# Adding an attention bias with accumulating transfers from DRAM instead of GpSimd additions

## The reference

```python
qkv = in_proj_weight[None] * x[:, None, :, :, :, None] + in_proj_bias[None]
q, k, v = (qkv[:, n].reshape(16, -1, 4) for n in range(3))
q, k = softplus(q), softplus(k)
s = cumsum(k[:, :, :, None] * v[:, :, None, :], axis=1)
z = cumsum(k, axis=1)
y = einsum('nsi,nsij->nsj', q, s) / einsum('nsi,nsi->ns', q, z)[:, :, None]
y = concatenate([ones_like(y[:, :1]), y[:, :-1]], axis=1)
y = sum(hid_proj_weight[None] * y[:, None], axis=-1) + hid_proj_bias[None]
y = sum(out_proj_weight[None] * tanh(y), axis=1) + out_proj_bias[None]
```

## Time and profile before

| | |
|---|---|
| median of 3 runs | 3651.82 us (3649.66 to 3657.69) |
| the profiled execution's own time | 3653.92 us |
| its span | 3652.1 us |
| busy in the span | PE 2039.0 us, DVE 1541.7, ACT 852.6, POOL 1682.0 |
| of POOL: the gathers of the second layer | 1089.1 us |
| of POOL: bias additions (line 956), 16 for each of the three parts | 72.7, 72.6 and 72.5 us |
| first and last projection of a value in the last stage | start at 2523.8 and 3524.9 us |
| granted clock of TensorE, mean | 0.758 of full speed |

### The profile page before, as it was taken

How to read it: one execution, slowest core, us unless ns; L and a number is a source line. 1 busy time by engine, 2 the same in 40 slices (tenths; PEclk the granted TensorE clock), 3 DMA queues, 4 the chain that set the end, 5 groups by cost and what they waited for, 6 DMA issues and landing times. The chain is left out here.

```text
span 3652.1 us, 36691 instructions
## 1 busy us (share of the span) xinstructions
PE 2039.0 (56%) x14480; PEld 1282.6 (35%) x14480; DVE 1541.7 (42%) x1349; ACT 852.6 (23%) x1117; POOL 1682.0 (46%) x1342
## 2 busy tenths in 40 slices
PE   3666323444544444444534444561788888888887
PEld 2544212222232222232322223351454544544545
DVE  3222420221122202220222112374788888878885
ACT  3111301021111112021111111252333233233241
POOL 0000075555655565555655575233454554554542
PEclk9877656666766666666766676786899899999899
DMA  7999442333323232323323232203111311212212
GB/s 322 431 432 431 155 114 83 89 89 89 92 84 91 85 96 85 92 84 91 91 83 92 84 97 84 100 17 105 55 61 55 103 60 66 95 57 67 96 52 78
DMA packets 169913, 423.39 MB, mean 116 GB/s; under 512 B 92648, under 2 KB 111232, under 8 KB 152704
## 3 DMA queue, kind: packets, MB, share of 16 engines
q1 hardware_dynamic: 114560, 271.53, 20.2%
q0 software_dynamic: 55296, 151.07, 13.8%
HBM read 396.91 MB, written 25.58 MB: 116 GB/s over the span
## 5 line engine op out<-in xcount | busy, mean ns | idle before, releaser
L436 POOL DMA_INDIRECT gath<-table,idx x1152 | 1089.1, 945 | 798.9 <-PE p_col L594 348.6
L594 PE MATMUL p_col<-ident,gath 128*128 128x128 f32 x2304 | 398.9, 338 | 667.2 <-issue 440.0
L594 PEld LDWEIGHTS p_col<-ident,gath 128*128 128x128 f32 x2304 | 342.8, 177 | 736.6 <-issue 632.4
L537 DVE TENSOR_TENSOR xt<-xt,p_y 128x512 f32 (+1 forms) x16 | 11.0, 688 | 1380.8 <-remote 1363.0
L483 ACT ACTIVATE cols<-p_col 128x384 f32<-128x384 f32 x384 | 186.0, 491 | 1162.1 <-remote 557.6
L582 PE MATMUL p_y<-cols,wreg 128*64 128x512 f32 x576 | 306.4, 692 | 141.2 <-issue 86.0
L535 DVE TENSOR_TENSOR gath<-gath,p_stat 128x2304 f32<-128x2304 f32 x128 | 317.5, 2549 | 64.4 <-DMA gath<-table,idx 62.6
L1192 PE MATMUL p_state<-xt,tri 128*128 128x512 f32 x512 | 257.4, 650 | 64.5 <-DVE prod L1080 64.5
L960 POOL TENSOR_TENSOR query<-query,expo 128x2048 f32<-128x2048 f32 x16 | 102.1, 6379 | 334.7 <-DVE query L1058 334.7
L1080 DVE TENSOR_TENSOR prod<-p_state,query 128x2048 f32<-128x2048 f32 x80 | 183.1, 2289 | 127.5 <-PE p_state L1197 127.5
L1228 PE MATMUL p_sum<-ident,prod 128*128 128x128 f32 x1024 | 171.0, 337 | 107.2 <-DVE prod L1102 107.2
(11 more groups left out here) (221 smaller groups left out, 2772.6 us busy)
## 6 DMA issues: line engine op xcount, KB each, us to landing
ring<-in_w SPq DMA_DIRECT2D x64, 2304.0 KB, 18.8
hidw<-in_hidw SPq DMA_DIRECT2D x64, 1024.0 KB, 4.8
gath<-table,idx POOLq DMA_INDIRECT x1152
table<-pix SPq DMA_DIRECT2D x256, 64.0 KB, 1.8
xt<-in_x SPq DMA_DIRECT2D x1, 4096.0 KB, 12.7
ring<-in_x SPq DMA_DIRECT2D x1, 4096.0 KB, 12.9
resid<-xt SPq DMA_DIRECT2D x32, 128.0 KB, 2.4
xlate<-resid SPq DMA_DIRECT2D x16, 256.0 KB, 2.9
```

Of the source, the lines that this page charges most:

```text
L436: nc.gpsimd.indirect_dma_start(out=gath[:, t % SLOTS, k].rearrange("p n c -> p (n c)"), out_offset=None, in_=entries[u], in_offset=bass.In ...
L594: last = nc.tensor.matmul(p_col[g][:, k], corners, ident[:], start=(r == 0), stop=(r == 1), is_transpose=True)
```

## The change

The bias is no longer kept in SBUF. `add_bias` becomes a transfer issued by POOL which reads the bias from DRAM and adds it to the tile where it lies. Each part gets a counter of its own that rises by 16 per transfer, and a counter `bias_begun` is raised by POOL ahead of each transfer.

```diff
-EARLY = {"inw": [P, 3 * ATT, HALF], "inb": [P, 3 * ATT, HALF]}
+EARLY = {"inw": [P, 3 * ATT, HALF]}
...
             def add_bias(part, n, scaled, b, done):
                 pool.wait_ge(scaled, b + 1)
-                tt(part[:], part[:], inb[:, n * A:(n + 1) * A], ALU.add).then_inc(done, 1)
+                pool.sem_inc(bias_begun, 1)
+                pool.dma_start(part[:], d["inb"][:, n * A:(n + 1) * A], accum_op=ALU.add).then_inc(done, 16)
...
                 add_bias(value, 2, v_scaled, b, v_ready)
-                add_bias(key, 1, k_scaled, b, biased)
-                add_bias(query[u], 0, q_scaled, b, biased)
+                add_bias(key, 1, k_scaled, b, key_biased)
+                add_bias(query[u], 0, q_scaled, b, query_biased)
...
             def exponential(part, b, g):
-                act.wait_ge(biased, b * 2 + (g + 1))
+                act.wait_ge(query_biased if g else key_biased, b * 16 + 16)
...
                 if j == 0:
                     dve.wait_ge(soft, b * 2 + 1)
-                    dve.wait_ge(v_ready, b + 1)
+                    dve.wait_ge(v_ready, b * 16 + 16)
```

More of the change, by code:

```diff
@@ L833, in layer3 @@
     tiles, early_in = early
-    inw, inb = (tiles[name] for name in EARLY)
+    inw = tiles["inw"]
     with ExitStack() as ctx:
@@ L879, in layer3 @@
         v_scaled = sem("v_scaled"); v_ready = sem("v_ready"); k_scaled = sem("k_scaled"); q_scaled = sem("q_scaled")
-        biased = sem("biased"); absd = sem("absd"); expd = sem("expd"); lifted = sem("lifted"); lost_ready = sem("lost_ready")
+        key_biased = sem("key_biased"); query_biased = sem("query_biased"); bias_begun = sem("bias_begun"); absd = sem("absd"); expd = sem("expd"); lifted = sem("lifted"); lost_ready = sem("lost_ready")
         logd = sem("logd"); relud = sem("relud"); soft = sem("soft")
```

## The result

The changed kernel takes 3754.32 us (median of 4 runs, 3750.56 to 3756.58), the kernel before 3654.41 us in the runs beside it. The ratio is 1.0273, with a 95% interval of 1.0256 to 1.0291. The forecast was 3750 us. The profiled execution took 3753.32 us, 99.4 us more than the one before.

What follows compares the result with a forecast made beforehand. The prediction took the last stage's path through the key's bias to bound the kernel: 15 bodies x 6.0 = 90 us plus 8 us ahead of the loop, 98 us more, giving 3750 us for the median; range 3668 to 3920.

Steps and rivals of the forecast that it cites:

- What bounds the stage, and what has slack: Last stage: only the key's bias is on the path, 4.66 us from projection to ACT; value and query have slack.
- DVE loses no neighbour: Last stage: removing GpSimd's additions does not speed up DVE, whose key projection already took 2.28 us beside them.
- SP's missing load: Stage before the last: SP no longer loads 3072 KB of bias; worth nothing.
- Key behind the value ahead of the loop: Batch 0, ahead of the loop: the key's transfer queues behind the value's and lands 8 us later.
- The key's transfer in a body: Each last-stage body: key reaches ACT 10.5 us after its projection against 4.66, so 5.8 us later.
- issue by GpSimd, with the start behind the wait: Key's transfer: GpSimd's issue costs 0.95 us, taken from a gather's issue.
- fixed part and bytes: Key's transfer: 2.0 us fixed plus two passes over the bytes at 300 GB/s, 7.0 us.
- collisions: Key's transfer: SP's xlate load and output store, 256 KB each, mostly run before the key's bytes; 0.5 us added.
- TensorE's clock: Fourth state's matmuls after PE's longer idle time: 0.2 us extra a body, at most 2.0 us at the lower clock level.
- slow adder: Last stage: adding is slower than its bytes, so the key queues behind the value's transfer; 3908 us, chance 0.34.
- price of a plain load: Key's transfer: the old value's read is hidden, key 1.64 us late a body; 3676 us, chance 0.14.
- faster case: Last stage: key lands in under 4.66 us, so PE idles less and keeps the upper clock; 3620 us, chance 0.03.

Runs made afterwards that it cites:

- e1: Changed kernel with only the key's bias added by GpSimd again, value and query still by transfer: +0.5 us over the kernel before, ratio 1.0000.
- e4: Kernel before, no transfers, but GpSimd adds the query's bias ahead of the key's: +112.1 us over the kernel before, ratio 1.0348.
- e10: Changed kernel with the value's transfer issued last and SP's xlate load held until the key has landed: +71.6 us over the kernel before, ratio 1.0190.
- e12: The changed kernel run again, on the chip of e9 to e11: +101.1 us over the kernel before, ratio 1.0272.
- e11: As e10, but the key's transfer overwrites instead of adding (leaves out the projected key): +29.8 us over the kernel before, ratio 1.0081.
- e7: Changed kernel, but SP stores the output first and loads xlate only when the key has landed: +89.4 us over the kernel before, ratio 1.0238.
- e9: Changed kernel with GpSimd issuing the key's transfer first, then query's, then value's: +74.8 us over the kernel before, ratio 1.0203.
- e8: Kernel before with GpSimd's key addition and ACT's absolute value and exponential cut in two halves that overlap: 3603.69 us, ratio 0.9883.
- e3: Changed kernel, but the key's transfer overwrites the tile instead of adding: +61.7 us over the kernel before, ratio 1.0189.
- first four runs: Key back on GpSimd, key alone by transfer, key's transfer plain, query first without transfers; on their chip the kernel before takes 3215.8 us.

## Why the prediction was right

*What bounds the stage, and what has slack.* Right, and shown by e1: with the key alone back on GpSimd the whole loss goes. That DVE loses no neighbour and that value and query stay covered stand in the same run. The rows that I had named for the first did not show it: in the earlier trace rows the value's addition ends at 3124.21, as the key's projection starts at 3124.15. That SP's missing load is worth nothing stands in the changed kernel alone: its last stage starts at 2525.8 us, not sooner than the 2523.8 of before. GpSimd was not left almost idle, as I had written; it is busy for 1505.7 us instead of 1682.0. e4 shows that the lateness is what is paid, since it costs the same with no transfer at all.

*Key behind the value ahead of the loop.* Forecast 8 us; the wait ahead of that `lost_part` grew from 11.9 to 19.6 us, the longest waits of the two fences above: 7.7 us.

*The key's transfer in a body.* 5.8 us late by the forecast, 5.24 us measured. Its terms were further off than their sum:

| term, us | forecast | measured | by |
|---|---|---|---|
| issue by GpSimd, with the start behind the wait | 0.95 | 0.58 + 0.86 | timeline of after |
| fixed part and bytes | 9.0 | 8.1 - 0.86 = 7.2 | e10 |
| collisions | 0.5 | 1.1 to 1.2 | changed kernel or e12 less e10 |

The bytes were the term sized wrongly. I took two passes at the software queue's mean of 300 GB/s, 7.0 us. That mean came from gathers of 1 KB rows, and the rows of 8 KB were nearer to the plain load's rate: 5.6 us by the queue's share, and 2.8 us for the second pass by e10 and e11. (That the length of the rows makes the difference was not tested.) The Trainium skill's rule for the adding transfers of a collective (Collectives: The Full Stack, The bandwidth ceiling), two reads and about half the rate, agrees with this: its ratio of 1.93 gave 5.4 us by estimate, nearer than my 7.0.

The collisions were sized too small. I had the value's bytes through at 3129.6 in the body of the earlier trace rows, about when the key's begin: by my own terms at 3126.43 + 2.95 = 3129.4, not at the 3128.5 that I wrote. That the value hardly holds the key's bytes was right. But I let SP's 512 KB run mostly ahead of the key's, and did not see that the value's transfer holds them back until the key's begins. The slices of after show the engines full across that point, and e7 and e9 show that either one removed takes away half or nearly all of it.

*TensorE's clock.* Forecast 0.2 us a body, measured 0.8: DVE's wait for the fourth state rose from 3.57 to 4.39 us on average. The step that failed was taking one row for the price. The 5.64 us of the earlier trace rows stood behind 6.63 us of idle time and 1.09 us of other matmuls, and was no bound:

```profile
3130.85 6.62 PE L1193 MATMUL p_state<-xt,tri 128*128 128x512 f32 x8 [7.66 <-DVE prod L1081]
```

This is the body of after with the longest fourth wait, 5.02 us, and its granted clock was 0.50 from 3130.85 to 3136.00, the lower level all through; for the 5.52 us of the body shown above it was 0.67. So the longer wait is the clock. In the changed kernel the fourth wait goes from 3.55 to 5.02 us between bodies whose waits ahead of `lost_part` differ by 2.2 us at most. e4, later still, stays at 3.91 to 4.30 us in all of its bodies. So the cost does not rise with the idle time, and what sets it from body to body stays open.

*Sum.* 5.24 + 0.8 = 6.0 us a body were forecast as 5.8 + 0.2. The errors of 1.8 us in bytes against 0.5, 0.6 and 0.6 in issue, collisions and clock cancelled, and that was luck: the mechanism and its place were right and shown, the 0.1% was not earned by its four sizes.

*Rivals.* The slow adder would have shown a key that lands with twice the bytes behind the value in each body; that happened only ahead of the loop. The price of a plain load rested on a hidden read of the old value; e10 and e11 show that read paid with 2.8 us. Only e11, which leaves the addition out, comes near to its 3676: 29.8 us over before, where it said 24. The Trainium skill's figure for a transfer from GpSimd (DMA: Bandwidth & Descriptors, Anatomy of one DMA), 4.4 us by estimate for 1024 KB, was not reached even by the plain one: 5.3 us in e11. Without the 0.86 us of its issue 4.4 us are left. The faster case was right about its second half only: e8 shows that a shorter idle time on PE keeps the matmuls at the upper level and gives 1.5 us a body.

*Left open.* In e3 the plain transfer behind the value's took 7.8 us and in e11 5.3 us, so it lost 2.5 us to sharing where the adding one lost 1.1 to 1.4. The two runs were on different chips. In e3's first body, with the value's transfer ahead but without SP's, it lost nothing (5.2 us), so the loss goes with SP's two; why it is larger than for the adding one wasn't tried.

## What to carry to other kernels

An operation can be moved off a busy engine for nothing only if what comes behind it does not wait for its result. Here 2 of 3 additions could go and one could not, and the waits of the one engine that bounds the stage (DVE idle 1.78 us ahead of `lost_part`) told which. The transfer that adds in place cost its plain landing plus one more pass over the bytes (8.1 against 5.3 us for 1024 KB), and started later behind its wait than an addition (0.58 against 0.08 us); for this size it fits where the result is needed 10 us later, not 5. And where a wait of the bounding engine is paid in full, cutting the work ahead of it in two, so that two engines overlap on it, gains what the wait has, here 1.7 us a body, and here 1.5 us of TensorE's clock as well.

## What the runs showed that was not expected

The same kernel took 3215.8 us on the chip of the first four runs and 3645.4 to 3654.4 us wherever else it ran. The difference lies ahead of the last stage: its first projection started at 2086 us there and at 2524 us here. The gathers' group shows it (busy, mean ns | idle before), first the kernel before:

```profile
L436 POOL DMA_INDIRECT gath<-table,idx x1152 | 1089.1, 945 | 798.9 <-PE p_col L594 348.6
```

and e1 on the faster chip:

```profile
L436 POOL DMA_INDIRECT gath<-table,idx x1152 | 1089.6, 946 | 386.9 <-issue 349.4
```

An issue takes 946 ns on both, but GpSimd's idle time between them is 387 instead of 799 us. 348.6 us of the 799 were waits for PE's `p_col`; on the faster chip these are 1.2 us. Why PE is later elsewhere was not looked into. So the time of a run is compared only with that of the kernel before on the same chip.
